# Feed-forward stage: index lists loaded once, the add of gathered rows moved from POOL to DVE; attention in edge blocks; gathers two tiles ahead; the new state turned one step later

## The reference

```
L0: q,k,v = x@qW, x@kW, x@vW;  s = sum(q[src]*k[dst])/sqrt(16) + edge_attr@eW
    attn = softmax of s over the edges of each dst;  out = segment_sum(v[src]*attn, dst)@oW
    x1 = LN(x + out);  h = gelu(LN(x1@f1W)) @ f2W;  x = LN(x1 + h)
L1: mean of x[src] per dst;  out = x@Wl.T + mean@Wr.T, divided by its norm
L2: h = x@lin.T;  three times: agg = segment_sum((h@W)[src], dst);  h = GRU(agg, h)
L3: mean of x[src] per dst;  [x, mean] @ weight
```

## Time and profile before

| | |
|---|---|
| time, median of 3 runs | 6024.28 us (6012.01 to 6027.09) |
| the profiled execution | 6028.9 us, its span 6027.0 us |
| busy share PE / DVE / ACT / POOL | 71% / 68% / 49% / 60% |
| POOL busy and PE clock in ffn (790 to 1900 us) | 954.36 of 1110 us, 0.96 |
| POOL busy and PE clock in attend (128 to 790 us) | 412.86 of 662 us, 0.81 |

### The profile page before, as it was taken

One profiled execution on the slowest core, in us unless ns is written; L12 is line 12 of the kernel. 1 busy time (PEld: TensorE's weight loads), 2 busy tenths in 40 slices (PEclk: granted clock), 3 DMA queues, 4 the chain that ended last, 5 costly groups with the idle time before them and its releaser, 6 DMA issues. The chain is left out here.

```text
span 6027.0 us, 75672 instructions
## 1 busy us (share of the span) xinstructions
PE 4279.1 (71%) x16190; PEld 2524.1 (42%) x16190; DVE 4070.7 (68%) x13522; ACT 2924.8 (49%) x6388; POOL 3629.7 (60%) x3234
## 2 busy tenths in 40 slices
PE   6577759999997556546665679967996669836643
PEld 3244434444443333334443445534443334336643
DVE  6576659999997444457775676557665889836633
ACT  0466637777775010146665345534443446536643
POOL 4676558888885888735555660056104757855355
PEclk8788869999998777778887899988998899977877
DMA  6233323333332444456665675457545667757621
GB/s 214 66 85 80 73 70 99 99 99 99 99 99 78 62 62 63 54 141 196 193 190 162 185 211 146 131 160 214 164 141 147 176 159 211 197 162 227 183 78 54
DMA packets 767598, 802.43 MB, mean 133 GB/s; under 512 B 139632, under 2 KB 527800, under 8 KB 767018
## 3 DMA queue, kind: packets, MB, share of 16 engines
q1 hardware_dynamic: 405354, 393.44, 23.5%
q0 software_dynamic: 117504, 209.42, 15.0%
q10 hardware_dynamic: 244288, 194.72, 9.7%
HBM read 445.32 MB, written 351.92 MB: 132 GB/s over the span
## 5 line engine op out<-in xcount | busy, mean ns | idle before, releaser
L462 PE MATMUL gate_bank<-gate_ht,gate_whh 128*128 128x512 f32 x1764 | 874.6, 618 | 32.5 <-DVE gate_n L532 22.2
L925 POOL DMA_INDIRECT xh<-mean_xh,mean_pos_all x392 | 378.0, 964 | 349.0 <-DVE mean_xh L1027 158.9
L462 PEld LDWEIGHTS gate_bank<-gate_ht,gate_whh 128*128 128x128 f32 x1764 | 341.3, 202 | 413.0 <-issue 381.6
L2053 PE MATMUL back_ps_sums<-back_same,back_rows 128*128 128x512 f32 x400 | 289.5, 890 | 285.7 <-DMA back_rows<-x_a,back_idx 285.7
L151 POOL DMA_INDIRECT ffn_rows<-att_sums,ffn_idx x392 | 409.0, 1043 | 114.8 <-issue 106.3
L289 POOL DMA_INDIRECT gate_rows<-h_a,by_pos x200 | 195.8, 979 | 433.3 <-POOLq L117 327.3
L1494 PE MATMUL ffn_ps_f<-ffn_hg,ffn_f 128*128 128x512 f32 x784 | 407.1, 616 | 46.4 <-ACT ffn_hg L1671 46.4
L458 PE MATMUL gate_bank<-by_rank,gate_win 128*128 128x512 f32 x882 | 435.1, 593 | 0.0
L1487 PE MATMUL ffn_ps_u<-ffn_xs_t,ffn_up_w 128*128 128x512 f32 x784 | 387.2, 596 | 1.1 <-issue 1.1
L583 ACT ACTIVATE gate_z<-gate_bank,gate_b_rz 128x512 f32<-128x512 f32 x294 | 201.5, 686 | 351.0 <-PE gate_bank L462 221.0
L2034 POOL DMA_INDIRECT back<-back_out,back_dest x200 | 324.3, 1621 | 68.0 <-issue 60.1
(11 more groups left out here) (270 smaller groups left out, 11984.1 us busy)
## 6 DMA issues: line engine op xcount, KB each, us to landing
mean_x<-x_a SPq DMA_DIRECT2D x196, 256.0 KB
back<-blank ACTq DMA_DIRECT2D x99, 264.0 KB, 4.6
mean_rows<-back SPq DMA_DIRECT2D x98, 264.0 KB
hp<-mean_xh SPq DMA_DIRECT2D x98, 264.0 KB
gate_x<-xh SPq DMA_DIRECT2D x98, 264.0 KB
gate_hot<-hot_rows SPq DMA_DIRECT2D x100, 256.0 KB
ffn_x<-in_x_in SPq DMA_DIRECT2D x98, 256.0 KB
ffn_xr<-in_x_in SPq DMA_DIRECT2D x98, 256.0 KB
```

What stands on the lines that cost most here:

```text
L462: last = nc.tensor.matmul(bank_[:, :], whh[:, c * D:(c + 1) * D], ht[:, t.slot4, :], start=not inputs, stop=True)
L925: nc.gpsimd.indirect_dma_start(out=g["xh"][:, :], out_offset=bass.IndirectOffsetOnAxis(ap=pos_all[:, t.n, j:j + 1], axis=0), in_=xh[:, t.n ...
L2053: last = nc.tensor.matmul(ps_sums[t.slot][:, :], rows[:, t.slot4, j, :], same[:, t.slot, j, :], start=j == 0, stop=j == J - 1)
```

## The change

1. ffn: the index list of all 98 tiles is loaded by one DMA ahead of the weights, instead of a small load per tile. `a` = rows + x is computed on DVE, behind z. On POOL the four gathers stand first in a step. xh is a scalar_tensor_tensor (its second input is the inverse deviation, broadcast) instead of a tensor_scalar.
2. attend: index lists, turned rows and stored results in blocks: edge 128j+p of a tile sits on partition p, so that PE's columns are contiguous; the store has pieces of 512 bytes instead of 2 KB.
3. Gathers in attend, gate1, gate2 and mean3 wait for the tile two before instead of four before.
4. gates: hn has four buffers, and PE turns it (and what follows: ht and h stores, the last norm) a step later.

```
     def gather(self, pool, t):
-        wait(pool, self.summed, t.n - 3)
+        wait(pool, self.summed, t.n - 3 if self.carries else t.n - 1)
...
-        d, hn = (f.sb(s, [P, 2, SUPER]) for s in ("d", "hn"))
+        d, hn = f.sb("d", [P, 2, SUPER]), f.sb("hn", [P, 4, SUPER])
...
-                if t := item_at(2):
+                if t := item_at(3):
                     wait(pe, h_done, t.n + 1)
                     wait(pe, out_done, t.n)
...
                     sp.dma_start(idx[:, t.slot4, :, :].rearrange("p j c -> p (j c)"),
-                                 nm_tile(g["by_dst"], t)).then_inc(idx_loaded[t.slot4], 16)
+                                 g["edge_blocks"][t.n]).then_inc(idx_loaded[t.slot4], 16)
...
-                    wait(pool, rows_turned, t.n - 3)
+                    wait(pool, rows_turned, t.n - 1)
...
-                        last = nc.tensor.matmul(ps_out[:, j * D:(j + 1) * D], edge_columns(att[:, t.slot, :])[:, j, :],
+                        last = nc.tensor.matmul(ps_out[:, j * D:(j + 1) * D], att[:, t.slot, j * P:(j + 1) * P],
                                                 ow[:, :], start=True, stop=True)
...
         @block.sync
         def _(sp):
+            sp.dma_start(idx[:, :, :], whole_list(g["ptr_dst"])).then_inc(idx_loaded, 16)
...
-                    wait_alone(sp, gathered[t.slot4], 64 * t.u4)
-                    sp.dma_start(idx[:, t.slot4, :], list_tile(g["ptr_dst"], t)).then_inc(idx_loaded[t.slot4], 16)
...
-                if t := tile_at(2):
-                    wait(pool, gathered[t.slot4], 64 * (t.u4 + 1))
-                    wait(pool, x_loaded[t.slot4], 16 * (t.u4 + 1))
-                    wait(pool, xh_done, t.n - 3)
-                    nc.gpsimd.tensor_tensor(flat(a[:, t.slot4, :, :]), flat(rows[:, t.slot4, :, :]),
-                                            flat(x[:, t.slot4, :, :]), ALU.add).then_inc(a_done, 1)
+                if t := tile_at(0):
+                    if t.n == 0:
+                        pool.wait_ge(idx_loaded, 16)
+                    wait(pool, a_done, t.n - 3)
+                    pool.nop(nofuse=True)
+                    for j in range(J):
+                        nc.gpsimd.indirect_dma_start(
...
-                        last = nc.vector.tensor_scalar(xh[:, t.slot4, j, :], a[:, t.slot4, j, :],
-                                                       mv[:, root_slot(t, LN1), LN1, j, 0:1], inverse(t, LN1)[:, j:j + 1],
-                                                       ALU.subtract, ALU.mult)
+                        last = nc.vector.scalar_tensor_tensor(
+                            xh[:, t.slot4, j, :], a[:, t.slot4, j, :], mv[:, root_slot(t, LN1), LN1, j, 0:1],
+                            inverse(t, LN1)[:, j:j + 1].broadcast_to([P, D]), ALU.subtract, ALU.mult)
...
+                if t := tile_at(2):
+                    wait(dve, gathered[t.slot4], 64 * (t.u4 + 1))
+                    wait(dve, x_loaded[t.slot4], 16 * (t.u4 + 1))
+                    wait(dve, xh_done, t.n - 3)
+                    nc.vector.tensor_tensor(flat(a[:, t.slot4, :, :]), flat(rows[:, t.slot4, :, :]),
+                                            flat(x[:, t.slot4, :, :]), ALU.add).then_inc(a_done, 1)
```

More of the change, by code:

```diff
@@ L415, in step @@
                     sums.store_hots(sp, e)
-                if final and (t := item_at(5)) and t.has:
+                if final and (t := item_at(6)) and t.has:
                     wait(sp, stored[t.m % 2], 16 * (t.m // 2 + 1))
@@ L420, in step @@
                                  ).then_inc(back_loaded[t.m % 4], 16)
-            over_items(5 if final else 0, step)
+            over_items(6 if final else 0, step)
             if initial:
@@ L431, in step @@
             def step(edges_at, item_at):
-                if final and (t := item_at(5)):
+                if final and (t := item_at(6)):
                     ln.rstd(nc, pool, t, y_done)
@@ L435, in step @@
                     sums.gather(pool, e)
-                if final and (t := item_at(6)) and t.has:
+                if final and (t := item_at(7)) and t.has:
                     wait(pool, ids_made, 1)
@@ L444, in step @@
                             in_=back_x[:, t.m % 4, j, :], in_offset=None).then_inc(back_scattered[t.m % 4], 16)
-            over_items(6, step)
+            over_items(7 if final else 0, step)
             if final:
@@ L498, in step @@
                     sums.sum(pe, e)
-            over_items(2, step)
+            over_items(3, step)
         @block.vector
@@ L548, in step @@
                                             ALU.add).then_inc(n2_done, 1)
-                if final and (t := item_at(2)):
+                if final and (t := item_at(3)):
                     wait(dve, out_done, t.n + 1)
@@ L572, in step @@
                                          ).then_inc(id_done, 1)
-                if final and (t := item_at(6)):
+                if final and (t := item_at(7)):
                     wait(act, stored[t.slot], 16 * t.u)
@@ L576, in step @@
                              [y[:, t.slot, j, :] for j in range(J)], y_done)
-                if not final and (t := item_at(2)):
+                if not final and (t := item_at(3)):
                     wait(act, h_done, t.n + 1)
-                    act.dma_start(ht_out[t.tile], hn[:, t.slot, :]).then_inc(ht_stored[t.slot], 16)
+                    act.dma_start(ht_out[t.tile], hn[:, t.slot4, :]).then_inc(ht_stored[t.slot4], 16)
                 if t := item_at(1):
@@ L602, in step @@
                     nc.scalar.activation(ht[:, t.slot4, :], ps_in[:, :], ACT.Copy).then_inc(ht_made, 1)
-                if final and (t := item_at(6)):
+                if final and (t := item_at(7)):
                     wait(act, y_done, t.n + 1)
                     act.dma_start(part_tile(x_out, t.tile, 0, D), y[:, t.slot, :, :]).then_inc(stored[t.slot], 16)
-            over_items(6 if final else 2, step)
+            over_items(7 if final else 3, step)
             for b in range(2):
                 act.wait_ge(stored[b], 16 * (NT // 2))
-                if not final:
-                    act.wait_ge(ht_stored[b], 16 * (NT // 2))
+            if not final:
+                for b in range(4):
+                    act.wait_ge(ht_stored[b], 16 * ((NT - b + 3) // 4))
 class Turn:
@@ L2209 @@
     src_row[:E] = inputs["src"]
+    arrays["edge_blocks"] = np.ascontiguousarray(
+        edges[1:].reshape(ET, J, P, 2).transpose(0, 2, 1, 3)).reshape(ET, P, 2 * J)
     arrays.update(x_in=x, edges=edges, edge_attr_t=edge_t, src_row=src_row)
```

33 lines of the change are left out of this document (18 added, 15 removed).

## The result

The changed kernel takes 5853.62 us in the median of 4 runs (5851.47 to 5861.99), the kernel before 6021.82. The ratio is 0.9725, its 95% interval 0.9708 to 0.9742: 168 us faster. Forecast were 5952 us and a range of 5895 to 6010.

A forecast was written before the change was run, and what follows sets the result against it. The prediction took ffn as the main term, POOL and DVE never stopping and blocking each other, PE close behind. From 6028.9 us, -88 (ffn), +10 (index list), +10 (attend), -5 (gates, mean3) gave 5956, 5952 for the median; range 5895 to 6010.

The forecast's parts named there:

- Three times 0.31: ffn: POOL's first three gathers each take 0.31 us more beside DVE's xh, z and a, 0.5 net per step.
- its own bounds: ffn: limits around the forecast -88 us, from -60 with POOL at 10.07 us a step to -115 with DVE at 9.42.
- the 3.12 us of xh: ffn: DVE's four xh lose 1.26 us for each tensor_tensor that POOL runs at that moment.
- the order keeps xb away from a: ffn: xb on POOL begins after the four gathers, when DVE has been through a for 2 us.
- Rival A: ffn: DVE's two-input operations stretch three gathers to 1.6 us each, an 11.15 us step, 6076 us in all; chance 0.04.
- PE, put at 9.1 to 9.9: ffn: PE's work per step lies between 9.1 and 9.9 us, close behind POOL in the forecast 9.8 us step.
- The gathers' wait for two tiles before costs nothing at these steps: attend: eight gathers take 10 us while two steps take 20.7 or more, so waiting two tiles before costs 0.
- the +10 for the clock: attend: less work and more idle time push PE toward its low clock level, +10 us, bounds 0 to 33.
- the out product itself isn't on the path: attend: the out product falls from 2.03 to 1.05 us, but the next q waits for ACT's copies, so no gain.
- turning later gives PE the same work: Second halves of gate0 and gate1: PE has no idle time to give, so the later turn gains nothing there.
- The allowance of +15 for late gathers: gates and mean3: gathers only two tiles ahead may come late on a full DMA, up to +15 us.
- a sign of being wrong: gate0 onward: the prediction would be wrong if these phases moved by over 30 us; it took -5.

The follow-up runs named there:

- e6_xh: The kernel before with only xh in ffn written as scalar_tensor_tensor, a staying on POOL, on chip 1: 6036.12 us, ratio 0.9971.
- e7_move: The kernel before with the ffn part (list loaded once, a on DVE, gathers first), but xh still a tensor_scalar: 5994.76 us, ratio 0.9911.
- e9_four: The changed kernel with gathers four tiles ahead again in attend, gate1, gate2 and mean3, on chip 10: 5900.78 us, ratio to before 0.9799.
- e4_blocks: The kernel before with only attend's edge blocks (contiguous columns, changed store) added, on chip 8: 5586.62 us, ratio 0.9995.
- e10_noblocks: The changed kernel with attend's edge blocks undone (strided columns again), on chip 10: 5856.99 us, ratio to before 0.9718.
- c_after3: The changed kernel, unchanged, run again on chip 8: 5476.06 us, ratio 0.9807 to before on that chip.

## Why the prediction was wrong

Its sum missed by 101 us of span: 30 in ffn, 30 in attend, 28 from gate0 on, 12 in mean1 and 3 in the list, less 2 in back1.

ffn, the term that was mis-sized. The step that failed is "After the change xh, z and a fill the first 2.9 us behind the power, and POOL's first three gathers lie there. Three times 0.31", which put POOL at 9.5 to 10. Beside xh, z and a the gathers take 1.02, 0.96 and 1.03 in the usual step. The 1.26 was taken for the price of lying beside z; but e6_xh has z in the same place and 1.01 us in 70 of 72 steps. So the sign was wrong: gathers got cheaper by 0.26 us a step. Which property of the new xh brings that is open, as said with e7_move, and with it why the price in before was 1.26. POOL and DVE meet at 9.42, the DVE bound the prediction had at 9.42, and -117 is what its own bounds called -115.

That the 3.12 us of xh are POOL's two tensor_tensors held (2.94 in the other form too). That the order keeps xb away from a held as well, though xb meets var, at 0.12 us a step. Rival A's mechanism, gathers stretched to 1.9 us by DVE, is in the chip's reach: one gather a step in e7_move, one step in 18 in the changed kernel. That it stayed rare was not derived by anything in the prediction. PE, put at 9.1 to 9.9, was no bound at 9.42.

attend. What failed is "The gathers' wait for two tiles before costs nothing at these steps". It was judged at a steady step and never at the start, where the trace of before has 42 us between the second and third q. On a chip with stalls it brings 21 us (e9_four). The other half of the miss is the +10 for the clock: the stage's clock is 0.80 for 0.81, and neither blocks alone (e4_blocks) nor blocks undone (e10_noblocks) shows any loss. So it is -20 instead of +10. That the out product itself isn't on the path held on chip 10; on chip 8 the blocks go with 6 us less in attend, in single executions.

The gates. That turning later gives PE the same work where it is full held, and so did gate2's unchanged DVE stretch; the turn is worth about 10 us. The allowance of +15 for late gathers was right on chip 8. On the first chip 28 us more were gained than forecast, and the phases from gate0 on moved by 33, which the prediction itself had named as a sign of being wrong. Going by chips 1 and 10, the turn gave 4 to 9 of gate1's and 4 to 8 of gate2's, the shorter filling about 3 and 8 more (10 in each, less what later steps lose). These are differences of single executions. The rest, gate0's 2 and mean3's 7, is within the spread of the same code there.

mean1's -12.5 belongs to no part of the change: the same code varies by 23 us on such chips.

On chip 8, where none of these stalls exist, the change measured -111, of which ffn's -117 and its list are nearly all. There the forecast of -72 misses by 39: 30 in ffn and some 16 in attend, which came out 6 us shorter instead of 10 longer, less some 8 in the gates (by the columns of c_after3 and the runs with one part). That the first measurement fell on a chip with stalls, and so gained 57 us more than chip 8 shows, is luck.

## What to carry to other kernels

Read the first steps of every phase as well as a steady one: a wait that costs nothing in the steady state can set the filling, and here, on the chips with stalls, the filling of three phases was worth 40 us before later steps took some back. When two engines block each other, change the form and the place of an operation apart, since either alone gave an eighth or a third of the gain; and look at what ends together with the stretched instruction, not only at what lies beside its start. And compare before on each chip anew: the same change was worth half as much again on one chip as on another.
